# A graph block whose edge additions read their weight row from SBUF in layers 1 to 3, and a third PSUM bank for taken rows

## What is computed

```python
xn = layernorm(x)
h = xn
for l in range(4):                                   # graph layers
    m = relu(h[src] + edge_weight * We[l] + be[l])   # 40000 x 512
    agg = segment_sum(m, dst, 1250)
    z = batchnorm(((1 + eps[l]) * h + agg) @ W1[l] + b1[l]) * gamma[l] + beta[l]
    h = relu(relu(z) @ W2[l] + b2[l])
x = x + h + linear_attention(xn)                     # 8 heads, Wq, Wk, Wv, Wp
x = x + mixture_of_8_experts(layernorm(x))           # top-1 routing, gelu, 512 -> 256 -> 512
```

## Time and profile before

| what | us |
|---|---|
| median of 3 runs | 1721.02 |
| lowest and highest of them | 1719.23, 1727.67 |
| span of the profiled execution | 2011.5 |
| PE busy in it | 1575.7 |
| DVE busy | 1309.7 |
| POOL busy | 1027.9 |
| ACT busy | 971.1 |
| mean granted TensorE clock (share of 2.4 GHz) | 0.887 |

### The profile page before, as it was taken

One profiled execution on the slowest core, in us unless ns is written; L12 is line 12 of the kernel. 1 busy time (PEld: TensorE's weight loads), 2 busy tenths in 40 slices (PEclk: granted clock), 3 DMA queues, 4 the chain that ended last, 5 costly groups with the idle time before them and its releaser, 6 DMA issues.

```text
span 2011.5 us, 22868 instructions
## 1 busy us (share of the span) xinstructions
PE 1575.7 (78%) x7214; PEld 688.0 (34%) x7214; DVE 1309.7 (65%) x2538; ACT 971.1 (48%) x1262; POOL 1027.9 (51%) x1070
## 2 busy tenths in 40 slices
PE   2767788869787787876888887877967887777968
PEld 1223333335442222332433232333423322324445
DVE  7667777776675676755585666675565775665644
ACT  3434444434435565554436556564345664564411
POOL 3766665665144566655056666662246665651033
PEclk8887888978889888988889998999888988989979
DMA  7655655665265566655166666662456665663733
GB/s 254 189 167 159 178 169 162 177 217 160 72 193 172 170 185 182 185 162 154 53 209 171 194 197 183 188 203 82 126 172 197 195 190 169 186 190 105 265 130 115
DMA packets 119099, 343.30 MB, mean 171 GB/s; under 512 B 20712, under 2 KB 24892, under 8 KB 118718
## 3 DMA queue, kind: packets, MB, share of 16 engines
q0 software_dynamic: 85248, 278.41, 47.8%
q1 hardware_dynamic: 32318, 60.78, 9.3%
q10 hardware_dynamic: 1408, 2.56, 0.5%
HBM read 323.61 MB, written 19.96 MB: 171 GB/s over the span
## 4 chain that ended last, share of the span: by engine, by line
PE 49%; DVE 19%; issue 11%; another core or an unknown queue 9%; ACT 8%; DMA 2%; DVEq 1%; POOL 1%; ACTq 0%; POOLq 0%
PE ps L1902 44%; DVE ring L1075 9%; ACT ring L1681 5%; PE ps L1975 3%; DVE lg L1131 2%; ACT zT L1726 1%; DVE aggT L1495 1%; DVE onehot L1066 1%; PE ps L2060 1%; ACT parts L1690 1%; DVE aggT L1132 1%; DVEq L1118 1%; DMA aggT<-pair_table,token_i 1%; DMA zT<-pair_table,token_i 0%
## 5 line engine op out<-in xcount | busy, mean ns | idle before, releaser
L878 POOL DMA_INDIRECT ring<-x_table,idxT x1014 | 985.4, 972 | 799.7 <-issue 274.7
L1075 DVE SCALAR_TENSOR_TENSOR ring<-ps,wT,ring 128x512 f32<-128x512 f32 x930 | 627.5, 742 | 7.3 <-issue 2.0
L1681 ACT ACTIVATE ring<-ring 128x1536 f32<-128x1536 f32 (+1 forms) x313 | 463.2, 1514 | 200.1 <-DVE ring L1075 141.0
L1902 PE MATMUL ps<-ring,onehot 128*32 128x512 f32 x2028 | 417.9, 683 | 102.9 <-ACT ring L1681 48.3
L1902 PE MATMUL ps<-ring,zT 128*128 128x512 bf16 x1080 | 298.8, 403 | 154.9 <-issue 105.1
L1726 ACT ACTIVATE zT<-ps 128x512 f32<-128x512 f32 x336 | 194.3, 599 | 366.6 <-PE ps L1902 206.8
L1131 DVE TENSOR_REDUCE lg<-ps 128x128 f32<-128x512 f32 x208 | 142.9, 687 | 288.2 <-PE ps L1975 127.6
L1902 PE MATMUL ps<-zT,xT 128*32 128x512 f32 (+2 forms) x752 | 221.2, 691 | 0.0
L1902 PEld LDWEIGHTS ps<-ring,zT 128*128 128x128 bf16 x1080 | 97.7, 100 | 303.0 <-issue 162.1
L1902 PEld LDWEIGHTS ps<-ring,onehot 128*32 128x32 f32 x2028 | 87.6, 118 | 312.4 <-issue 253.3
L1902 PE MATMUL ps<-aggT,w 128*128 128x256 f32 (+2 forms) x512 | 154.9, 455 | 13.1 <-DVE aggT L1132 9.6
(11 more groups left out here) (328 smaller groups left out, 1408.3 us busy)
## 6 DMA issues: line engine op xcount, KB each, us to landing
ring<-x_table,idxT POOLq DMA_INDIRECT x1014
zT<-slot_table SPq DMA_DIRECT2D x36, 312.5 KB
w<-in_L_gnn_W SPq DMA_DIRECT2D x8, 1024.0 KB
ring<-in_L_ffn_W SPq DMA_DIRECT2D x16, 512.0 KB, 9.7
x_table<-ring SPq DMA_DIRECT2D x24, 250.0 KB
x_table<-ring SPq DMA_DIRECT2D x9, 256.0 KB
stage<-in_x ACTq DMA_DIRECT2D x9, 256.0 KB
pair_table<-mix SPq DMA_DIRECT2D x9, 256.0 KB
```

The lines of the kernel that those rows point to most:

```text
L878: gp.indirect_dma_start(out=to, out_offset=None, in_=table[:, :], in_offset=bass.IndirectOffsetOnAxis(ap=idx, axis=0)).then_inc(done, 16)
L1075: ins = v.scalar_tensor_tensor(out=at[:, u, :], in0=terms[:, :], scalar=wT[:, c, u:u + 1], in1=at[:, u, :], op0=ALU.mult, op1=ALU.add)
L1681: a.activation(at, at, ACT.Relu).then_inc(relu_done, 1)
L1902: return nc.tensor.matmul(o, lhsT, rhs, start=start, stop=stop)
```

## The change

In layers 1 to 3 the additions read `we_bc` in SBUF. The copy into ps6 is gone, with its wait on `terms_ready`; DVE waits for the load of `we_bc` itself. `TAKES` becomes 3, so that takes use ps4, ps5 and ps6 in turn, a take waits for the relu of the take three before it, and the split of a step's takes into first and later ones becomes 3 and 0, 3 and 1, 3 and 0 where it was 2 and 1, 2 and 2, 2 and 1. Layer 0 keeps its copy in ps5.

```diff
-    TAKES = 2
+    TAKES = 3
     def tiles_of(l, j):                 # unchanged, its result is not
         ...
         return tiles[:TAKES], tiles[TAKES:]

-        def terms_bank(l):
-            return ps[6] if l in MIXED else ps[5]
+        def terms_of(l, j):
+            return ps[5] if l not in MIXED and j >= TERMS_FROM else we_bc
         def take_bank(l, T):            # unchanged, its result is not
             return ps[4 + T % TAKES]

             def add_tiles(l, j, tiles):
-                terms = terms_bank(l) if l in MIXED or j >= TERMS_FROM else we_bc
+                terms = terms_of(l, j)
                 ...
             def messages(l):            # DVE
-                if l in MIXED:
-                    v.wait_ge(terms_ready, l + 1)
-                else:
-                    v.wait_ge(we_loaded, 16)
+                v.wait_ge(we_loaded, l * 16 + 16)

-            def terms_copy(l):          # ACT
-                a.wait_ge(we_loaded, l * 16 + 16)
-                a.activation(terms_bank(l)[:, :], we_bc[:, :], ACT.Copy).then_inc(terms_ready, 1)
+            def terms_copy():
+                a.wait_ge(we_loaded, 16)
+                a.activation(ps[5][:, :], we_bc[:, :], ACT.Copy).then_inc(terms_ready, 1)
             def first_pieces(l):
                 ...
                     mid_piece(l, t - 1)
-                    if t == 1:
-                        terms_copy(l)
```

More of the change, by code:

```diff
@@ L1828, in beside @@
                         a.wait_ge(q_ready, QS)
-                        terms_copy(l)
+                        terms_copy()
                     if kind == "q":
```

## The result

The changed kernel takes 1765.26 us (median of 4 runs, 1758.52 to 1767.66) against 1720.40 for the kernel before (4 runs, 1719.23 to 1727.67): a ratio of 1.0238, 95% interval [1.0204, 1.0271], +44.9 us. The forecast was +18 us. The time lies in the range, and it is the rival "everywhere" that came true (about 1768).

What follows compares the result with a forecast made beforehand. The prediction took POOL's gather issue to bound the gather stretches, within 2%, with PE and ACT close behind. Its terms summed as 19 + 0 + 0 - 1 = +18 us, 1739 us, with a range of 1702 to 1770.

Steps and rivals of the forecast that it cites:

- everywhere: Rival: POOL leads in all 108 steps of layers 1 to 3, +37 to +56 us, about 1768; chance 0.10.
- What bounds the kernel: Gather stretches: POOL within 2% of the bound, 7.5 us a chunk against 7.10 for PE with ACT without early pieces.
- surplus of 290 us: Profiled span 2011.5 us against the runs' median 1721.0; read as mostly pauses of the profile's own in the gather stretches.
- Part 1: DVE's 708 additions read SBUF: 747 ns against 743 each, taken as nothing, 2.8 us if uncovered.
- Part 2: POOL's gathers beside additions from SBUF take longer: 0.34 us per train, ends 0.02 and 0.52.
- Part 3: Share on the path: 57 steps without early pieces at 0.34 us give 19 us; the steps with early pieces give 0.
- Part 4: Third take bank on PE and ACT: gain of 1 us at the layers' starts, as POOL is the later loop.
- 47.4 us of the earlier trace: PE's idle time before takes that names their relus; the upper end of the third bank's gain.
- Part 5: Dropping ACT's three copies into ps6, about 0.6 us each, from the making of the pieces: 0, at most 2 us.
- Hidden: Rival: the longer gathers disappear in slack because PE's loop sets the timed pace; 1721 us, within 5; chance 0.24.
- faster: Rival: PE with ACT sets the pace and takes wait less for relus, gaining 31 us: 1690; chance 0.21.
- The lock: Rival: a gather meeting a train waits it out, 2.5 us, one per train in 57 steps: +144, 1865; chance 0.03.

Runs made afterwards that it cites:

- terms_only: Changed kernel with two take banks and the old take order: 1761.63 us, ratio 1.0240 on the quick chip; repeated on a long chip (terms_only_2), 0.9848.
- the kernels with five gathers: Kernel before, terms_only and changed kernel, each without tile 5's gather in 102 chunks of layers 1 to 3: 0.9440, 0.9272, 0.9218 on a first long chip.
- half_sbuf: Kernel before, with tiles 3 to 5 of each chunk in layers 1 to 3 added from SBUF, tiles 0 to 2 from PSUM: 1755.83 us, ratio 1.0197.

## Why the prediction was wrong, step by step

**What bounds the kernel.** The sentence that POOL is within 2% of the bound of the gather stretches (1.276 us a gather against 1.252) came near to the truth on the quick chip (270.9 of about 285 us, and no wait behind a layer's first chunks), but by luck: it came from an argument that was wrong. I read the surplus of 290 us as mostly the profile's own. It fits a long chip, and the profile of before on the quick chip has nothing of it. About 38 us of the surplus also lie outside the gather stretches, where the argument put none. Having set the pauses aside as artefacts for the sum, I still used rows that they shape.

**Part 1** held: 744 ns an addition, trains of 4.05 to 4.07 us. (The additions are 702 and 3 more, not 708.)

**Part 2** held in kind. L878's mean rose from 960 to 1032 to 1036 ns, inside the 1010 to 1050 that were forecast, with typical gathers at 0.94 to 1.02. The term was somewhat mis-sized: I took 0.34 us a train and measured 15.8 / 36 = 0.44.

**Part 3 is the step that failed**: "About 19 steps per layer are without early pieces ... in the other 17 per layer POOL has 2 us to spare, which covers it: 0." The 2 us were the earlier trace rows, taken on a long chip. On the quick chip POOL runs through such steps with 0.30 us between gathers, so the steps with early pieces pay like the others, and all 36 of a layer count. The prediction had the alternative in its own words (the cover may be only pauses; then 108 x 0.34 = 37, at most 56). And its own bound spoke for it: if POOL works 1.252 of every 1.276 us, it has 0.14 us to spare per chunk of six on average, and can't have 2 us in 17 of 36 steps. With 108 steps and 0.44 us the sum is 48 us against 44.9 measured. Between the forecast's 19 and 48, the share on the path makes 17 us (51 x 0.34), and the price of a train 11 (108 x 0.10).

**Part 4** was right for this chip: the third bank brought nothing (terms_only 1.0240, the change 1.0238). The 47.4 us of the earlier trace rows were not there. On long chips it may bring 10 to 14 us, in the kernels with five gathers.

**Part 5** held: no row of the pieces' making moved.

**The rivals.** "Hidden" and "faster" describe the long chips: POOL's extra work costs nothing there, and the time falls. But "faster" put the gain down to the third bank, and on the long chips most of it comes with the source of the additions (0.9848 for terms_only_2). Both rest on waits that the earlier trace rows showed truly for one chip. "The lock": one gather of 4.65 us in three layers, against one per train.

**The rule weighed.** The gathers grew, by 0.07 us and more, where the Trainium skill (SBUF — State Buffer, "Who interferes with whom") infers that `tensor_tensor`, which takes only the read interface of the shared pair, leaves descriptor generation alone. The growth sits above all in the gathers that start inside a train: in half_sbuf those already running when an addition from SBUF began kept 0.947 on the mean (69 of them), while 106 started inside had 1.23. In the changed kernel those already running had 1025 ns (79 of them), beside 986 ns in the kernel before (83), where the additions read PSUM. The same section states a full block for the whole instruction for the 2-port modes; 1.02 us beside additions of 0.74 agrees that this is not one.

## What to carry to other kernels

Before a share is put on the path, set the engine's whole pitch (work plus the issue gap) against the period of a timed execution; if the two differ by 2% on average, no large part of the stages can have much slack, whatever one profile's timeline shows. When the span of a profile is far from the median of the runs, don't call the difference an artefact and go on using its waits: profile once more, or price the change for both worlds. And an addition of DVE with two tensors in SBUF has a price on GpSimd's indirect DMAs (here 968 to 1017 ns on the mean), so a constant operand in PSUM is worth its bank as long as GpSimd leads.

## What the runs showed of the hardware that was not expected

- The same kernel takes 1716 to 1728 us on one chip and has medians of 2036 to 2047 on three others. Most of the difference between the two profiles of before lies in the gather stretches (1611.5 us against 1352.6; the rest 400.0 against 362.4): POOL's waits for slots there, and time of PE with no cause named (179.1 us against 1.2). One change had opposite signs on the two, 1.0238 and 0.9748, both with intervals that exclude 1.
- An indirect DMA that GpSimd starts inside a train of additions from SBUF takes 1.02 us, often 1.3 to 1.5, once 4.65, against 0.95. The first of a train pays most: halving the additions kept 76% of POOL's excess. It isn't special to the additions: in the kernel before, quick chip, the gathers that overlap line L1161, a `tensor_scalar` from SBUF to SBUF, have a mean of 1.05 us (46 of them), and those beside no work of DVE 0.95 (61).
- On the long chips two extra memsets a chunk on POOL never cost anything; in one of four runs they gained 1.35% [0.81, 1.89], in another 0.49% [0.13, 0.86]. I have no cause for that.
